# Moving ternary weight chunks, weight loads and rotation tables around the K projection of a fused attention and ternary layer

## What is computed

```python
def layer(x):                     # x: [1, 8192, 2048]
    x = x + attn(layernorm(x))
    x = x + ffn(layernorm(x))

def attn(h):
    q, k, v = split(h @ Wqkv, 3)
    q, k = rmsnorm(q, q_norm_w), rmsnorm(k, k_norm_w)   # over all 2048 channels
    q, k = rope(q, cos, sin), rope(k, cos, sin)         # 16 heads of 128
    mask = (q_idx >= k_idx) & (q_idx - k_idx <= 1023)
    return softmax(mask(q @ k.T / sqrt(128))) @ v @ Wo

def ffn(h):
    x_q = ternary(h, 0.33, 0.5)
    w_q = ternary(weight, 0.2, 0.6)
    return x_q @ (w_q + rram_variation).T
```

## Time and profile before

| | us |
|---|---|
| median of 3 runs (1113.26 to 1115.31) | 1113.59 |
| the profiled execution | 1115.65 |
| its span, slowest core (core 1) | 1114.1 |
| spans of the eight cores | 1101.3 to 1114.1 |
| TensorE busy, core 1 | 1036.1 (93%) |
| VectorE busy | 738.3 (66%) |
| ScalarE busy | 453.9 (41%) |
| GpSimd busy | 205.1 (18%) |

### The profile page before, as it was taken

The page is one execution under the profiler, slowest core; times in us unless marked ns, Lnnn a source line. Parts: engine busy times, 40 slices in busy tenths (PEclk is TensorE's granted clock), DMA queues, the critical chain, the costliest instruction groups (busy, mean ns, idle before and its releaser), DMA issues.

```text
span 1114.1 us, 20483 instructions; the slowest of 8 cores (1101.3 to 1114.1 us)
## 1 busy us (share of the span) xinstructions
PE 1036.1 (93%) x6796; PEld 547.6 (49%) x6796; DVE 738.3 (66%) x1286; ACT 453.9 (41%) x737; POOL 205.1 (18%) x222
## 2 busy tenths in 40 slices
PE   0899999999999969999999789899899899999998
PEld 0454444444444424444444466666666644444443
DVE  2783344578697865378887599999999756662211
ACT  1785333333233323221111599999999800000000
POOL 0012000000000000001000256666666500000000
PEclk9999999999999989999999799999999999999999
DMA  8987789744868666728200022554226272116322
GB/s 158 299 272 126 158 171 210 172 84 123 204 174 218 187 212 149 176 84 190 108 22 18 23 78 78 130 175 112 43 73 103 43 259 39 38 38 217 105 76 76
DMA packets 57386, 145.43 MB, mean 131 GB/s; under 512 B 21698, under 2 KB 25794, under 8 KB 53314
## 3 DMA queue, kind: packets, MB, share of 16 engines
q1 hardware_dynamic: 45858, 103.19, 28.7%
q0 software_dynamic: 11424, 40.90, 21.2%
HBM read 147.21 MB, written 26.21 MB: 156 GB/s over the span
## 4 chain that ended last, share of the span: by engine, by line
PE 71%; DVE 9%; issue 9%; DMA 6%; ACT 4%; DVEq 0%; ACTq 0%; POOL 0%; SPq 0%; POOLq 0%
PE ps L446 20%; PE ps L455 19%; PE ps L640 10%; PE ps L558 10%; PE ps L582 4%; PE ps L527 3%; PE ps L596 3%; DVE RW L899 3%; DMA RB<-wfT 2%; DMA RW<-wqkv 2%; DMA RB<-rrT 2%; DVE tmp L790 1%; ACT RC L742 1%; ACT RW L736 1%; PE ps L482 1%
## 5 line engine op out<-in xcount | busy, mean ns | idle before, releaser
L455 PE MATMUL ps<-RA,RW 128*128 128x512 bf16 x1536 | 334.0, 380 | 11.1 <-ACT sq L704 11.1
L455 PEld LDWEIGHTS ps<-RA,RW 128*128 128x128 bf16 x1536 | 150.4, 98 | 194.1 <-issue 14.4
L446 PE MATMUL ps<-RW,RA 128*128 128x512 bf16 x1024 | 224.9, 380 | 0.0
L899 DVE TENSOR_SCALAR_CACHE_REDUCE RW<-ps 128x1152 f32<-128x1152 f32 x128 | 173.1, 1352 | 20.0 <-PE ps L530 14.5
L446 PEld LDWEIGHTS ps<-RW,RA 128*128 128x128 bf16 x1024 | 99.7, 98 | 117.8 <-issue 0.8
L416 POOL TENSOR_SCALAR RW<-RW,rinv 128x1152 bf16<-128x1152 bf16 x86 | 105.2, 1223 | 141.7 <-DVE rinv L913 141.1
L527 PE MATMUL ps<-RB,RC 128*128 128x512 bf16 (+1 forms) x384 | 110.2, 334 | 20.6 <-DVE RW L899 12.2
L843 DVE TENSOR_TENSOR ps<-ps,sq 128x512 f32<-128x512 f32 x90 | 62.6, 696 | 84.5 <-ACT sq L704 84.5
L558 PE MATMUL ps<-RB,RC 128*128 128x512 bf16 x512 | 111.2, 379 | 0.0
L736 ACT ACTIVATE RW<-RW,negm 128x1152 bf16<-128x1152 f32 x86 | 108.5, 1262 | 0.0
L377 POOL DMA_DIRECT2D RW<-wqkv x48 | 26.0, 560 | 339.7 <-PE ps L455 326.9
(11 more groups left out here) (100 smaller groups left out, 1128.4 us busy)
## 6 DMA issues: line engine op xcount, KB each, us to landing
RW<-wqkv POOLq DMA_DIRECT2D x48, 512.0 KB, 14.2
RB<-x_all SPq DMA_DIRECT2D x16, 1024.0 KB, 6.9
RB<-wfT SPq DMA_DIRECT2D x24, 512.0 KB, 7.3
RB<-rrT SPq DMA_DIRECT2D x24, 512.0 KB, 8.1
RB<-wo POOLq DMA_DIRECT2D x16, 512.0 KB, 5.4
RA<-x_all SPq DMA_DIRECT2D x8, 1024.0 KB, 7.7
y<-sq SPq DMA_DIRECT2D x32, 256.0 KB, 2.4
ffhbm<-stg SPq DMA_DIRECT2D x14, 512.0 KB, 7.9
```

Of the source, the lines that this page charges most:

```text
L446: m = e.matmul(bank(g % 3), xlnT(d, 128 * t, 128), wslot(b)[:, 512 * d:512 * (d + 1)], start=(d == 0), stop=(d == 15))
L455: m = e.matmul(bank(g % 3), wslot(b)[:, 512 * d + 128 * hh:512 * d + 128 * (hh + 1)], xlnT(d, tok, 512), start=(d == 0), stop=(d == 15))
L899: e.tensor_scalar(out=sm(i), in0=scores(i), scalar1=-1.0, scalar2=None, op0=ALU.mult, op1=ALU.min, accum_out=negm[:, i % 4:i % 4 + 1]).the ...
```

## The change

Three edits:

1. `NFF_B` goes from 48 to 44, and the slots change. Chunks 14 and 15 are hung on groups 49 and 51, which had none. Of groups 53 to 95 that have no rope, only group 64 still has two chunks; before, groups 64, 76, 83, 90, 92, 94 and 95 had two. Groups 97 to 108 have one chunk each (12), where eight of them had one (8). The boundary of the buffers and the wait ahead of group 96 follow `NFF_B`.
2. The second to fourth quarters of the weight blocks `b` = 6, 7 and 8 (K's second to fourth block) wait for 3, 6 and 9 groups more than the first.
3. In SyncE's loop over V's stores, the four pieces of K's cosines and sines are issued ahead of the wait and the store of the same `g`.

```diff
-NFF_B = 48
+NFF_B = 44
@@ def plan():
         ROPEQ_AT[53 + 36 * p // 15] = p
+    slots += [49, 51]
     for g in range(53, 96):
         if g not in ROPEQ_AT:
-            slots += [g] * (2 if g in (64, 76, 83, 90, 92, 94, 95) else 1)
-    slots += [97, 98, 100, 102, 103, 105, 107, 108]
+            slots += [g] * (2 if g == 64 else 1)
+    slots += list(range(97, 109))
@@ SyncE
             for g in range(V1, V3):
                 c, t = 1 + (g - V1) // 16, g % 16
-                e.wait_ge(pj_free, g + 1)
-                e.dma_start(out=vhbm[c][:, 512 * t:512 * (t + 1)], in_=vstg(g)).then_inc(v_spill[g % 4], 16)
                 if g < V1 + 4:
                     ...
+                e.wait_ge(pj_free, g + 1)
+                e.dma_start(out=vhbm[c][:, 512 * t:512 * (t + 1)], in_=vstg(g)).then_inc(v_spill[g % 4], 16)
@@ GpSimd, w_load(b)
                 for k in range(4):
+                    if 6 <= b <= 8 and k:
+                        e.wait_ge(pj_mm, BLOCKS[b - 2][2] + 3 * k)
```

## The result

| | before | changed |
|---|---|---|
| median, us | 1113.53 | 1100.69 |
| the profiled execution, us | 1115.65 | 1100.83 |
| its span, slowest core | 1114.1 (core 1) | 1099.3 (core 3) |
| spans of the eight cores | 1101.3 to 1114.1 | 1093.7 to 1099.3 |

The ratio is 0.9883, with a 95% interval of 0.9868 to 0.9897: 12.8 us less. The forecast was 1101.5.

What follows compares the result with a forecast made beforehand. Bound: VectorE must finish chunk `NFF_B - 1` before K's last block may be written. Waits and clock, 12.6 us, gone and 0.5 back make 12.1: profiled 1115.65 becomes 1103.5, median 2.1 lower, 1101.5 us; range 1099 to 1107.5.

Steps and rivals of the forecast that it cites:

- the first term: TensorE's waits at groups 99 and 89 and the clock lost after: 9.70 + 1.35 + 1.57 = 12.6 us gone.
- One step ahead of group 89: VectorE's chunks ahead of group 89: four fewer (8.4 us), so TensorE's 1.35 us wait there goes.
- Six chunks fewer are enough with all waits for loads kept: Groups 53 to 96: 12.6 us less VectorE work, chunk 43 done at 388.4, group 99's wait gone with 1.3 us to spare.
- Without the waits VectorE keeps up: Groups 53 to 95: VectorE on time at group 95, chunk 43 done at about 384.9, 4.8 us to spare at group 99.
- Chunks 14 and 15: At groups 49 and 51: VectorE's idle time hides the first, the second leaves 0.5 us for later slack; cost nothing.
- Paced quarters: K's weight blocks: VectorE's load waits ahead of group 96 shrink from 15.8 us to 0 to 3; no gain by itself.
- The last block: K's groups after 96: late loads put VectorE 11 us behind; costs TensorE between nothing and 4 us, taken as 0.5.
- The Trainium skill's rule of turns between queues: DMA engines alternate queues by packet; were that all, load 25 lands as chunk 50 begins and the 0.5 us is 0.
- K's tables: VectorE's first table gains at most 2 us, the last stays tied to TensorE's groups; cost and gain nothing.
- The first one: Rival: loads 25 to 27 land later, TensorE waits 2 to 9 us in groups 109 to 114; 1103.5 to 1110; chance 0.24.
- "under 2 us": Sign ahead of group 96: ScalarE should wait under 2 us there.
- The slowest core's extra time behind the first scores: Rival: the slowest core's extra time after the projections is absent in other runs, giving 1097 to 1100 us; chance 0.07.

Runs made afterwards that it cites:

- eight chunks put back: Changed kernel with second chunks at groups 83, 85, 87, 88, 90, 92, 94, 95 again (NFF_B 52, four chunks behind group 96): 0.9979 of before, median 1111.0 us.
- the chunks alone: Kernel before with only the first edit (NFF_B 44, new slots, chunks 14 and 15 at groups 49 and 51): 0.9893 of before, median 1102.0 us.

## Why the prediction was right

**The bound and the first term.** The wait at group 99 was set by the date of the last chunk ahead of group 96, and both waits went as whole terms. The sum said 9.70 + 1.35 + 1.57 = 12.6 us gone and 0.5 back. The trace has 392.6 - 380.7 = 11.9 net; with the new 0.89 us added back, 12.7 gone. The 1.57 us of clock are in it: the long wait of eight chunks put back has the clock at 0.50 and 1.5 us more behind it than the short ones of 1.27 and 1.96 us, which have no slow matmuls behind them. One step ahead of group 89 was miscounted: only two chunks fewer stand there (the second ones of groups 76 and 83), not four, so 4.2 us and not 8.4. That is still more than the 1.35 us, and the wait went.

**Six chunks fewer are enough with all waits for loads kept.** The run of the chunks alone shows it. Its margin was larger than the 1.3 us of the prediction, 4.9 us: chunk 43 released ScalarE at 383.77, with group 52 started at 227.51; shifted to the clock of the trace before (1.06 us later) that is 384.8, not 388.4. The subtraction kept every microsecond of waiting as lateness at group 96. The four waits of the earlier trace rows were not all there was (with the one below and two of 0.2 us it is 17.7), 13.0 of them were left, and VectorE's slack behind the last of them, at 348.67, took up the rest.

```profile
346.51 0.69 DVE L805 SCALAR_TENSOR_TENSOR stg<-RB,tmp 128x512 bf16<-128x512 f32 x1 [1.40 <-DMA RB<-rrT]
```

**Without the waits VectorE keeps up.** Chunk 43 was forecast for 384.9 and freed ScalarE at 384.08, in a trace 0.8 us ahead: 384.8.

**Chunks 14 and 15.** Hidden, as said. The sum of group 52 started at 233.25, 5.44 us after the group's first matmul; before it was 233.63 - 228.57 = 5.06. The 0.4 us went into VectorE's slack.

```profile
233.25 0.69 DVE L846 TENSOR_TENSOR ps<-ps,sq 128x512 f32<-128x512 f32 x1
```

**Paced quarters: margin, no gain of their own.** Right for the kernel as changed, since the chunks alone have the gain already. Read as a statement on pacing it would be wrong: alone it gains 10.4 us. Two causes with one effect were both removed, and only the run of each alone tells that either would all but have done. The forecast of 0 to 3 us of waits ahead of 96 held.

**The last block.** The mechanism was right and the sizes were off in both directions. `rrT` of load 25 was forecast to take 19.1 us and took 15.2; that of load 26 was forecast to land by 428.2, 19.1 us after its issue, and took 21.6. So VectorE waited 6.28 us in chunk 50, not 11, and 8.3 more in chunk 52. The margin that gave way was that of group 111 (2.2 us in the prediction), by 0.89 us; I had taken 0.5 for all. The bounds of 0 to 4 us held: over the eight cores the largest such wait was 1.3 us, and in the two profiles of the changed kernel six and four cores had none.

**The Trainium skill's rule of turns between queues** ("DMA: Bandwidth & Descriptors", section "Queues, rings and completion order") would have had no lag in chunk 50 and no new wait. The landings of 15.2 and 21.6 us are against that use of it, but not against turns as such. From 410 to 418 us the two queues moved all but the same number of packets (below), as turns packet by packet would give; over the 20 us of the earlier trace rows it was 458 against 737, and that was not taken apart. What the estimate left out was the rest of SyncE's queue: from 402 to 418 us it moved 1.62 MB, and the pair is 1.05 MB. A store of 512 KB was issued right behind the pair, at 402.22. No run takes that store away, so its part in the 15.2 us is not shown.

```profile
q0 software_dynamic: 248, 0.89, 65.1%
q1 hardware_dynamic: 250, 0.91, 39.3%
```

**K's tables.** Nothing, as said. Alone, the edit moved the first table by 2.0 us against TensorE's groups, the 2 that I allowed, and the second by nothing.

**The rivals.** The first one, waits in groups 109 to 114, happened in kind and stayed under its 2 us. I had written that I would be wrong if TensorE waited there; the sign came, at 0.89 us, and since the sum itself had 0.5 us for such waits it was set too strictly. So was "under 2 us" for ScalarE ahead of group 96: it was 2.88, of which 2.28 are its usual wait for TensorE. The slowest core's extra time behind the first scores did not go away; another core took its place, and the profiled execution of the changed kernel lies 2.7 us under its forecast of 1103.5 for that reason and the earlier start. The median is 0.8 us from the forecast. That it is so near is in part luck: the change's own part was 0.2 us smaller than the 12.1 forecast, and 0.9 us came from what the sum does not hold.

## What to carry to other kernels

Ask of a wait by which date it would be gone, and then list everything that moves the producer towards that date. Once one edit is inside it, the others are margin: their gains don't add, and a profile after both can't say which one worked. A producer's idle time is worth removing only as far as the bound engine feels it; here, in the last block, 14 us of it were worth at most 1.

## What the runs showed that I had not expected

**Buffers swallow most of a producer's lateness, up to an edge.** ScalarE's wait at group 96 of 2.9, 9.0 and 11.4 us went with 0, 1.3 and 8.3 us at TensorE. The last step is large for the small difference, because ScalarE's wait is counted from when it became free, and it became free later in the last case: its start moved from 390.63 to 396.61, 6.0 us, or 7.1 counted from the start of group 52 (228.21 and 227.12 in these two traces); TensorE's wait grew by the same 7.1.

**Part of the spread of the cores was this wait.** TensorE's waits in the projections before ran from 6.2 us (core 5) to 11.3 (core 3); the spans ran over 12.8 us. After, they run over 5.6. With each core's own wait taken off, the spans before still run over 8.8 us (1094.2 on core 0 to 1103.0 on core 1), so the wait is not all of it.

**Attention runs in one of two rhythms on a core.** Between 600 and 880 us of the same execution of the changed kernel, TensorE's waits for VectorE and ScalarE on core 1 and then on core 3 are:

```profile
PE ps L530 <- DVE RW L902: 12.3, 35, 1.0
PE ps L585 <- ACT RC L745: 10.3, 29, 1.1
```

```profile
PE ps L530 <- DVE RW L902: 7.8, 19, 1.6
PE ps L585 <- ACT RC L745: 7.5, 28, 1.0
```

From its first scores to its end, a core in the first rhythm takes 493.0 to 493.8 us and one in the second 489.7 to 490.8. Among cores 1 to 7 the first was core 1 alone in the profile before, and cores 1, 2 and 4 after. What chooses the rhythm was not tried and stays open.
